# Cross attention in a decoder layer: keys and key steps turned side by side in one tile

## The chip, the core and the metric

The kernel runs on one NeuronCore of one Trainium2 chip. A core has TensorE (PE in the profile, PEld is its weight load), VectorE (DVE), ScalarE (ACT), GpSimd (POOL) and SyncE (SP), whose queue issues all transfers here. Times are device microseconds (us) of the whole program; lower is better.

## The reference, cut to what matters

One decoder layer on 32 batch elements of 100 rows by 256: a retention block, a cross attention, a feed-forward block, each with layer norm and residual. The change lies in the cross attention alone.

```python
kv_r = _apply_rope(kv_c, sin_k[None], cos_k[None])       # 1444 keys of 64 for each batch element
q_r = jnp.einsum('bshq,hqr->bhsr', q_big, W_qr)
k_r = jnp.einsum('bld,hdr->bhlr', kv_r, W_kr)
scores = jnp.einsum('bhsr,bhlr->bhsl', q_r, k_r)
attn = jax.nn.softmax(scores, axis=-1)
ctx_c = jnp.einsum('bhsl,bld->bhsd', attn, kv_r)
ctx_lat = jnp.einsum('bhsd,hkd->bhsk', ctx_c, w_kc_kv)
ctx = ctx_lat.transpose(0, 2, 1, 3).reshape(Bv, Sv, H * K)
return ctx @ Wo.T
```

There are 16 heads, so 1600 query rows meet 1444 keys in each batch element.

## The kernel before

An earlier phase leaves in device memory the rotated keys (`d["kr"]`), the differences of a key and its predecessor in another chunk (`d["kd"]`, called steps here), and the queries folded with W_kr, in a rounded part (`qh`) and a rest (`ql`).

The cross phase (`phase_cross_attention`) goes over the 32 batch elements in **slots**, one each, with an extra slot -1 ahead. A slot n does two things at once: the attention of element n, and the row maxima of element n + 1, which need rounded keys `kh`. It has 12 **chunks** c = 0 to 11 of 120 or 121 keys. For every chunk TensorE makes scores in two halves (`scores`, L1872), by adding to the scores in PSUM those of the chunk's steps (`dh` rounded, `dl` the rest; products dh by qh, dl by qh, dh by ql). ScalarE takes the exponentials (L1688), TensorE multiplies the chunk before with the values (`context`, L1892), and GpSimd adds the exponentials up (L1667), which gives the denominators.

Between these stand the **units** of the PSUM ring, which has two banks (0 and 1). `Ring` gives each single unit the next bank in turn; a unit waits until what was last in its bank has been read:
- `max` (L1940): two matmuls, both banks, read by one VectorE reduction (L1793).
- `half` twice (L1947): one matmul and bank each; the first is read by VectorE (L1802), the second is copied out by ScalarE (L1712), then reduced by VectorE (L1806).
- `kT` 0, 1, 2 (L1900): four transposes each; a third of the keys turned to 64 by keys. The tile `kr` holds each key twice side by side, so the turned keys stand in partitions 0 to 63 and again in 64 to 127, where the two halves of the queries need them. ScalarE copies them to `kh` (L1696).
- `dT` 0, 1, 2 (L1900): the same for the steps (`kd`, chunk 0 from `kr`); ScalarE copies to `dh` (L1703), VectorE subtracts for `dl` (L1770).
- `den` 0, 1 (L1925): sums of the denominators over partitions; ScalarE copies to `dens` (L1719).
- `mT` (L1952): the maxima, turned; they come back by way of device memory as `mq` for the first chunk of the next slot (L1879).
- `out` (L1931): the output product of the element before, 8 fp32 matmuls which the trace shows as 16; VectorE adds the residual (L1784).

TensorE's order is written by hand in `order`: out, dT 0 and kT 2 open chunk 0; dT 1 and 2 end chunk 2; den 0 and 1 end chunk 4; mT, kT 0 and kT 1 (for the element two slots on) end chunk 11. Chunks 0, 3 and 5 have no `half` pair; the last chunk's `max` is 466 wide, the others 512.

SyncE's queue runs `slot` in order: load_q, load_kv, load_xr, store_x2, load_qm, load_kr (two copies of the keys, after kT 2), load_kd (two copies of the steps, after dT 2), `invert`, load_m. `invert` (L1581) stores the denominators of the element before, waits, loads them as 100 by 16 (`few`), waits for VectorE's reciprocal (L1776), stores that, waits, and loads it spread over partitions (`rden`). VectorE takes this reciprocal in order, after the reduction of chunk 6, wherever the load is by then. GpSimd's `normalise` (L1653) multiplies context and `rden` after it has added chunk 9.

Of the kernel before, what the change touches and what calls it, by code (L numbers as in the profile page):

```python
# [18 lines left out]
L, DC = 1444, 64  # L19
# [1278 lines left out]
class Ring:  # L1298
# [18 lines left out]
    def count(self, units, where, keys=None):  # L1317

        totals = {("filled", i): 0 for i in range(2)} | {("read", i): 0 for i in range(3)}
        for n, u in enumerate(units):  # L1320
            totals["filled", self.banks[u][-1]] += 1
            totals["read", self.reader(u)] += 1
            where[keys[n] if keys else u] = dict(totals)
        return totals
# [48 lines left out]
def phase_cross_attention(nc, d, ahead):  # L1373


    with ExitStack() as ctx:
# [17 lines left out]
        kd = sb("kd", [LP, LC - 1, 2, DC])  # L1394
# [43 lines left out]
        first_max, *_, last_max = [u for u in units if u[0] == "max"]  # L1438
        copied = [u for u in units if u[0] == "half" and u[3] == 1]
        last_steps = [u for u in units if u[0] == "dT"][-2:]  # L1440


        def made(n, u):
            if u[0] == "kT":
# [7 lines left out]
        ends += [(B, ("out",)), (B, ("den", 0)), (B, ("den", 1)), (B + 1, ("out",))]  # L1452
        rg = Ring(ctx, nc, "x_ring", units, [("kT", 0), ("kT", 1)], ends, B - 2)
# [18 lines left out]
        kr_loaded = sig("kr_loaded", 32)  # L1472
        kd_loaded = sig("kd_loaded", 32)
# [6 lines left out]
        dh_copied = sig("step_high_copied", 3, 3)  # L1480
# [37 lines left out]
        def _(sp):  # L1518

            def load_kr(n):  # L1520

                if not is_at(n, 0):
                    wait_filled(sp, n - 2, ("kT", 2))
                rows = d["kr"][bass.ds(n, 1)].rearrange("b p (c e) -> (b p) c e", e=DC)
                for side in range(2):
                    sp.dma_start(kr[:, :, side], rows).then_inc(kr_loaded.sem, 16)

            def load_kd(n):

                if not is_at(n, 0):  # L1530
                    wait_filled(sp, n - 2, ("dT", 2))
                rows = d["kd"][bass.ds(n, 1)].rearrange("b p (c e) -> (b p) c e", e=DC)
                for side in range(2):
                    sp.dma_start(kd[:, :, side], rows).then_inc(kd_loaded.sem, 16)
# [62 lines left out]
            def slot(n, parity):  # L1597
# [22 lines left out]
            load_kd(0)  # L1620
# [16 lines left out]
        def _(pool):  # L1637
# [9 lines left out]
            def normalise(n):  # L1647
# [3 lines left out]
                wait_filled(pool, n, ("out",))  # L1651
# [24 lines left out]
        def _(act):  # L1676
# [14 lines left out]
            def copy_keys(n, i):  # L1691

                u = ("kT", i)
                wait_filled(act, n, u)
                a, b = span[i]
                act.copy(kh[:, a:b], ring[:, rg.banks[u][0], 0:b - a]).then_inc(read_sem(u), 1)  # L1696

            def copy_steps(n, parity, i):

                u = ("dT", i)  # L1700
                wait_filled(act, n, u)
                a, b = span[i]
                act.copy(dh[:, parity, a:b], ring[:, rg.banks[u][0], 0:b - a]).then_inc(dh_copied.sem, 1)  # L1703
# [23 lines left out]
            def slot(n, parity):  # L1727

                def singles(units):
                    for u in units:  # L1730
                        if not made_at(n, u):
                            continue
                        if u[0] == "kT":
                            copy_keys(n, u[1])
                        elif u[0] == "dT":
                            copy_steps(n, 1 - parity, u[1])
                        elif u[0] == "den":
                            save_den(n, u[1])

                for c in range(LC):  # L1740
# [3 lines left out]
                    if c == 0:  # L1744
                        singles(beside[c])
# [3 lines left out]
                    if c > 0:  # L1749
                        singles(beside[c])  # L1750
                    elif not is_at(n, -1) and not is_at(n, 0):
                        save_context(n)

            for i in range(2):
                copy_keys(-2, i)
# [6 lines left out]
        def _(dve):  # L1762
            ahead.wait(dve)

            def low_steps(n, parity, i):

                dve.wait_ge(dh_copied.sem, dh_copied.at(n, i + 1))
                u = ("dT", i)
                a, b = span[i]
                dve.tensor_tensor(dl[:, parity, a:b], ring[:, rg.banks[u][0], 0:b - a], dh[:, parity, a:b].bitcast(F32),  # L1770
                                  ALU.subtract).then_inc(read_sem(u), 1)
# [72 lines left out]
        def _(pe):  # L1844
# [15 lines left out]
            def scores(n, parity, c, u):  # L1860
# [35 lines left out]
            def turn(bank, i, chunk):  # L1896
# [480 lines left out]
```

## Time and profile before

| | us |
|---|---|
| three runs: lowest, median, highest | 2560.36, 2560.82, 2561.19 |
| the profiled execution, its own time | 2560.71 |
| its span, first to last instruction | 2558.9 |
| outside the span | 1.8 |
| cross phase, slots 0 to 30 (of the span) | 1479.5 |
| granted TensorE clock, mean | 0.964 |

The 1.8 us outside the span are a constant. The slots 0 to 30 begin with the first scores at 837.53 and end at 2317.05; slot 31 has no maxima to make. A row of a timeline gives start, duration, engine, line, operation and tiles; "[0.33 <-DVE x_x L1784]" is the idle time ahead of it and who ended that.

### The profile page before, as it was taken

To read this page: it belongs to the slowest core of one execution; us is meant where nothing else is said; L and a number is where in the kernel's file an instruction comes from. 1 tells how busy PE (TensorE), PEld (TensorE's weight loads), DVE (VectorE), ACT (ScalarE), POOL (GpSimd) and SP (SyncE) were. 2 spreads that over 40 slices of the span, in tenths; PEclk is the share of its full clock that TensorE was granted. 3 is DMA by queue.
4 is the path that set the end of the run, shared out by engine and by line. 5 is a ranking of instruction groups with operands and counts; after the bars stand their busy time and mean duration, and the time that the engine had idled before them with its cause. 6 is when DMAs were issued, how large, how long until landed. Compare 5 with 4: busy or idle time off the path is not lost. (4 is left out here: it accounts for less than half of the span.)

```text
span 2558.9 us, 47949 instructions
## 1 busy us (share of the span) xinstructions
PE 2353.3 (92%) x15794; PEld 1493.1 (58%) x15794; DVE 1620.2 (63%) x2689; ACT 1178.7 (46%) x1893; POOL 1840.6 (72%) x827
## 2 busy tenths in 40 slices
PE   7889858999985999999999999999999999999398
PEld 4455446777752555555555555555555555555288
DVE  5898857888855556556566566556565565561475
ACT  3232321222221556566565555555555555664143
POOL 2445526988871788888888888888888888889111
PEclk9999978999996999999999999999999999999699
DMA  4000016666653432332332432432432432410111
GB/s 132 14 22 22 13 51 177 185 173 183 183 162 83 87 78 64 90 76 64 91 75 64 94 72 64 94 74 61 96 75 59 98 74 58 98 46 13 39 46 39
DMA packets 310370, 210.37 MB, mean 82 GB/s; under 512 B 200054, under 2 KB 289354, under 8 KB 310176
## 3 DMA queue, kind: packets, MB, share of 16 engines
q1 hardware_dynamic: 310304, 209.51, 33.2%
q8 instruction: 38, 0.62, 0.1%
q14 instruction: 28, 0.23, 0.0%
HBM read 149.98 MB, written 59.48 MB: 82 GB/s over the span
## 5 line engine op out<-in xcount | busy, mean ns | idle before, releaser
L1667 POOL TENSOR_TENSOR x_acc<-x_acc,x_prob 120x1600 f32<-120x1600 f32 (+1 forms) x320 | 1153.1, 3603 | 42.8 <-ACT x_prob L1688 20.2
L1688 ACT ACTIVATE x_prob<-x_scores 120x800 f32<-120x800 f32 (+1 forms) x768 | 602.1, 837 | 41.6 <-PE x_scores L1872 19.7
L1892 PE MATMUL x_context<-x_prob,x_kv 120*64 120x400 f32 (+1 forms) x3072 | 600.4, 512 | 0.0
L1793 DVE TENSOR_REDUCE x_mx<-x_ring 115x2 f32<-115x1024 f32 (+2 forms) x384 | 467.7, 1218 | 202.3 <-PE x_ring L1940 189.8
L1892 PEld LDWEIGHTS x_context<-x_prob,x_kv 120*64 120x64 f32 (+1 forms) x3072 | 186.3, 136 | 254.1 <-issue 237.0
L1712 ACT COPY x_half<-x_ring 115x466 f32<-115x466 f32 (+2 forms) x288 | 153.4, 533 | 318.3 <-PE x_ring L1947 318.3
L1802 DVE TENSOR_REDUCE x_mx<-x_ring 115x1 f32<-115x466 f32 (+2 forms) x288 | 179.1, 622 | 182.7 <-PE x_ring L1947 182.7
L1872 PE MATMUL x_scores<-x_qh,x_dh 64*120 64x400 f32 (+1 forms) x1536 | 276.0, 355 | 0.0
L1872 PE MATMUL x_scores<-x_ql,x_dh 64*120 64x400 f32 (+1 forms) x1536 | 266.4, 341 | 0.0
L1872 PE MATMUL x_scores<-x_qh,x_dl 64*120 64x400 f32 (+1 forms) x1536 | 265.6, 341 | 0.0
L1667 POOL TENSOR_TENSOR x_acc<-x_prob 121x1600 f32<-121x1600 f32 x32 | 115.3, 3603 | 172.1 <-ACT x_prob L1688 172.1
L1806 DVE TENSOR_REDUCE x_mx<-x_half 115x1 f32<-115x466 f32 (+2 forms) x288 | 177.9, 618 | 12.7 <-ACT x_half L1712 11.8
L1940 PE MATMUL x_ring<-x_kh,x_qm 64*115 64x512 f32 (+2 forms) x768 | 161.4, 414 | 16.5 <-DVE x_dl L1770 7.7
L1947 PEld LDWEIGHTS x_ring<-x_kh,x_qm 64*115 64x115 f32 (+1 forms) x576 | 51.2, 175 | 191.6 <-DVE x_mx L1793 191.6
L1872 PEld LDWEIGHTS x_scores<-x_qh,x_dh 64*120 64x120 f32 (+1 forms) x1536 | 140.2, 178 | 36.6 <-issue 29.9
L1931 PE MATMUL x_ring<-x_wco,x_ctxn 128*100 128x256 f32 x560 | 135.8, 398 | 20.5 <-POOL x_ctxn L1653 14.6
L1947 PE MATMUL x_ring<-x_kh,x_qm 64*115 64x466 f32 (+2 forms) x576 | 134.2, 462 | 13.2 <-DVE x_mx L1793 13.2
L1872 PEld LDWEIGHTS x_scores<-x_qh,x_dl 64*120 64x120 f32 (+1 forms) x1536 | 140.3, 178 | 6.1
L1784 DVE TENSOR_TENSOR x_x<-x_ring,x_xr 100x256 f32<-100x256 f32 x35 | 14.8, 424 | 200.5 <-PE x_ring L1931 200.5
L1872 PEld LDWEIGHTS x_scores<-x_ql,x_dh 64*120 64x120 f32 (+1 forms) x1536 | 140.4, 178 | 1.1
L1215 PE MATMUL q_pp<-q_rot,q_ac 128*64 128x400 f32 x768 | 136.2, 503 | 1.0 <-issue 1.0
L1146 DVE TENSOR_TENSOR q_rot<-q_pq,q_cosq 128x400 f32<-128x400 f32 (+1 forms) x192 | 109.6, 571 | 31.1 <-PE q_pq L1203 28.0
(177 smaller groups left out, 3739.9 us busy)
## 6 DMA issues: line engine op xcount, KB each, us to landing
x_kr<-scratch_kr SPq DMA_DIRECT2D x64, 363.0 KB
x_kd<-scratch_kd SPq DMA_DIRECT2D x64, 332.8 KB
x_rden<-scratch_rden SPq DMA_DIRECT2D x68, 200.0 KB, 3.5
scratch_qh<-q_qsh SPq DMA_DIRECT2D x64, 200.0 KB, 3.8
scratch_ql<-q_qsl SPq DMA_DIRECT2D x64, 200.0 KB, 3.8
x_qm<-scratch_qh SPq DMA_DIRECT2D x64, 200.0 KB, 4.1
x_qh<-scratch_qh SPq DMA_DIRECT2D x64, 200.0 KB, 3.4
x_ql<-scratch_ql SPq DMA_DIRECT2D x64, 200.0 KB, 3.8
```

The source lines that it names most:

```text
L1215: mm = pe.matmul(pp[DC * side:DC * side + DC, p % 2, 0:GT], ac[:, 2 * p + side, j], rot[:, p % 4, 3 * side + j], start=j == 0, stop=j == 2)
L1667: pool.tensor_tensor(acc[0:rows, parity], first, prob[0:rows, c % PR], ALU.add).then_inc(acc_done.sem, 1)
L1688: act.activation(prob[0:rows, c % PR, u * HALF:(u + 1) * HALF].rearrange("p (j s) -> p j s", j=2), psc[0:rows, u, :, 0:BANK], ACT.Exp).the ...
L1712: act.copy(half[rows, k % 2, 0:b - a], ring[rows, rg.banks[u][0], 0:b - a]).then_inc(read_sem(u), 1)
L1793: dve.tensor_reduce(best[0:block_rows(r), :, r, i], ring[0:block_rows(r), :, 0:b - a], AX.X, ALU.max).then_inc(read_sem(u), 1)
L1802: dve.tensor_reduce(to, ring[0:block_rows(r), rg.banks[u][0], 0:b - a], AX.X, ALU.max).then_inc(read_sem(u), 1)
L1806: dve.tensor_reduce(to, half[0:block_rows(r), copied.index(u) % 2, 0:b - a], AX.X, ALU.max).then_inc(half_read.sem, 1)
L1872: mm = pe.matmul(psc[0:rows, u, j, 0:BANK], k[part, parity, a:a + rows], q[part, parity, cols], start=c == 0 and k is dh and q is qh, stop ...
L1892: mm = pe.matmul(pav[DC * s:DC * s + DC, j, 0:BANK], kv[0:rows, parity, c], prob[0:rows, c % PR, cols], start=c == 0, stop=c == LC - 1)
L1931: mm = pe.matmul(ring[0:S, bank, 0:E], ctxn[:, h // 4, (h % 4) * S:(h % 4 + 1) * S], wco[:, h], start=h == 0, stop=h == H // 2 - 1)
L1940: mm = pe.matmul(ring[0:block_rows(r), t, 0:b - a], qm[part, 1 - parity, r * MR:r * MR + block_rows(r)], kh[part, a:b], start=True, stop=True)
L1947: mm = pe.matmul(ring[0:block_rows(r), bank, 0:b - a], qm[part, 1 - parity, r * MR:r * MR + block_rows(r)], kh[part, a:b], start=True, sto ...
```

## The change

- `kr` holds in its two columns of 64 a key and its step, no longer the key twice. The tile `kd` is gone. A unit `turn` i replaces kT i and dT i: four transposes put keys in partitions 0 to 63 and steps in 64 to 127 of one bank.
- ScalarE copies the steps to dh[64:128], waits for VectorE, copies the keys to kh[0:64]. VectorE copies the keys to kh[64:128], waits for ScalarE, subtracts to dl[64:128]. A turn's bank is free when both are through.
- The lower halves of dh and dl are filled by two transfers within on-chip memory, `double_steps`, on SyncE's queue after `invert`.
- turn 2 ends chunk 4, after den 0 and 1. turn 0 and 1 end chunk 11. The unit out stands behind mT in chunk 11, ahead of them, and so handles its element at the end of a slot, not at the start of the next.
- Chunk 0 has no ring unit. Chunk 3 has a `half` pair; the last `max` is 512 wide.
- load_kr makes three transfers (keys, steps, the keys of chunk 0 once more) after turn 2; load_kd is gone.

```diff
-    own = [("out",), ("dT", 0), ("kT", 2)] if c == 0 else []
-    if c not in (0, 3, 5):
+    own = []
+    if c not in (0, 5):
         r, i = next(narrow)
         own += [("half", r, i, 0), ("half", r, i, 1)]
-    own += [("scores", 0), ("scores", 1), next(wide) if c < LC - 1 else ("max", *next(narrow)), ("context",)]
-    own += {2: [("dT", 1), ("dT", 2)], 4: [("den", 0), ("den", 1)],
-            LC - 1: [("mT",), ("kT", 0), ("kT", 1)]}.get(c, [])
+    own += [("scores", 0), ("scores", 1)]
+    if c > 0:
+        own.append(next(wide))
+    own.append(("context",))
+    own += {4: [("den", 0), ("den", 1), ("turn", 2)],
+            LC - 1: [("mT",), ("out",), ("turn", 0), ("turn", 1)]}.get(c, [])
...
 def load_kr(n):
     if not is_at(n, 0):
-        wait_filled(sp, n - 2, ("kT", 2))
+        wait_filled(sp, n - 2, ("turn", 2))
     rows = d["kr"][bass.ds(n, 1)].rearrange("b p (c e) -> (b p) c e", e=DC)
-    for side in range(2):
-        sp.dma_start(kr[:, :, side], rows).then_inc(kr_loaded.sem, 16)
-
-def load_kd(n):
...
+    steps = d["kd"][bass.ds(n, 1)].rearrange("b p (c e) -> (b p) c e", e=DC)
+    sp.dma_start(kr[:, :, 0], rows).then_inc(kr_loaded.sem, 16)
+    sp.dma_start(kr[:, 1:, 1], steps).then_inc(kr_loaded.sem, 16)
+    sp.dma_start(kr[:, 0, 1], rows[:, 0]).then_inc(kr_loaded.sem, 16)
+
+def double_steps(n, parity):
+    wait_read(sp, n - 1, ("turn", 2))
+    for t in (dh, dl):
+        sp.dma_start(t[0:DC, parity].bitcast(F32), t[DC:P, parity].bitcast(F32)
+                     ).then_inc(steps_doubled.sems[parity], 16)
...
     if further:
         load_qm(n + 2, parity)
         load_kr(n + 2)
-        load_kd(n + 2)
     invert(n)
     if not last:
+        double_steps(n + 1, 1 - parity)
         load_m(n + 1, 1 - parity)
...
+def copy_turn(n, parity, i):                      # ScalarE
...
+    act.copy(dh[DC:P, parity, a:b], ring[DC:P, bank, 0:b - a]).then_inc(dh_copied.sem, 1)
+    act.wait_ge(kh_copied.sem, kh_copied.at(n, (2, 3, 1)[i]))
+    act.copy(kh[0:DC, a:b], ring[0:DC, bank, 0:b - a]).then_inc(read_sem(u), 1)
...
+def take_turn(n, parity, i):                      # VectorE
...
+    dve.tensor_copy(kh[DC:P, a:b], ring[0:DC, bank, 0:b - a]).then_inc(kh_copied.sem, 1)
+    dve.wait_ge(dh_copied.sem, dh_copied.at(n, (2, 3, 1)[i]))
+    dve.tensor_tensor(dl[DC:P, parity, a:b], ring[DC:P, bank, 0:b - a],
+                      dh[DC:P, parity, a:b].bitcast(F32), ALU.subtract).then_inc(read_sem(u), 1)
```

SyncE's queue in the loop over slots, before, from the loads of keys on (ISA and REGISTER_ALU rows are waits and their values):

```order
L1526 DMA x_kr<-scratch_kr 121x12x64 x2
L59 REGISTER_ALU
L1534 ISA
L1534 DMA x_kd<-scratch_kd 121x11x64 x2
L59 REGISTER_ALU
L1585 DMA scratch_den<-x_dens 2x800
L1587 ISA
L1588 DMA x_few<-scratch_den 100x16
L1590 DMA scratch_rden<-x_few 100x16
L1593 DMA x_rden<-scratch_rden 64x800 x2
L59 REGISTER_ALU
L1575 DMA scratch_m<-x_mrow 14x115
```

The same place in the changed kernel:

```order
L1529 DMA x_kr<-scratch_kr 121x12x64
L1530 ISA
L1530 DMA x_kr<-scratch_kd 121x11x64
L1531 DMA x_kr<-scratch_kr 121x64
L59 REGISTER_ALU
L1589 DMA scratch_den<-x_dens 2x800
L1591 ISA
L1592 DMA x_few<-scratch_den 100x16
L1594 DMA scratch_rden<-x_few 100x16
L1597 DMA x_rden<-scratch_rden 64x800 x2
L59 REGISTER_ALU
L1537 DMA x_dh<-x_dh 64x1444
```

The key loads still stand ahead of the chain of `invert`, but what they wait for has moved from chunks 0 and 2 to the end of chunk 4, where the denominators come too.

TensorE's queue from the end of one slot to the first scores of the next, before (two transposes or more of a shape make one row):

```order
L1952 MATMUL x_ring<-x_ident,x_negm 14x115
L1912 ISA
L1900 MATMUL x_ring<-x_ident,x_kr 128x121 x4
L1900 MATMUL x_ring<-x_ident,x_kr 128x120 x4
L59 REGISTER_ALU
L59 ISA
L1931 MATMUL x_ring<-x_wco,x_ctxn 100x256 x4
L59 REGISTER_ALU
L1931 MATMUL x_ring<-x_wco,x_ctxn 100x256 x4
L1900 MATMUL x_ring<-x_ident,x_kr 128x121
L1900 MATMUL x_ring<-x_ident,x_kd 128x121 x3
L59 ISA
```

and in the changed kernel:

```order
L1939 MATMUL x_ring<-x_ident,x_negm 14x115
L59 ISA
L1920 MATMUL x_ring<-x_wco,x_ctxn 100x256 x4
L59 REGISTER_ALU
L1920 MATMUL x_ring<-x_wco,x_ctxn 100x256 x4
L59 REGISTER_ALU
L1906 ISA
L1892 MATMUL x_ring<-x_ident,x_kr 128x121 x4
L59 REGISTER_ALU
L1892 MATMUL x_ring<-x_ident,x_kr 128x120 x4
L1857 ISA
L1859 ISA
```

Sixteen transposes stood there (four more 128x120 follow the excerpt of before); eight stand there now, behind the output product.

VectorE's queue around the reciprocal, before (chunks 4 to 7):

```order
L1793 TENSOR_REDUCE x_mx<-x_ring 115x2 x2
L1802 TENSOR_REDUCE x_mx<-x_ring 115x1
L1806 TENSOR_REDUCE x_mx<-x_half 115x1
L1793 TENSOR_REDUCE x_mx<-x_ring 115x2
L1776 RECIPROCAL x_few<-x_few 100x16
L1802 TENSOR_REDUCE x_mx<-x_ring 115x1
L1806 TENSOR_REDUCE x_mx<-x_half 115x1
L1793 TENSOR_REDUCE x_mx<-x_ring 115x2
```

and in the changed kernel:

```order
L1785 TENSOR_REDUCE x_mx<-x_ring 110x2
L1760 CAST x_kh<-x_ring 64x480
L1762 TENSOR_TENSOR x_dl<-x_ring,x_dh 64x480
L1785 TENSOR_REDUCE x_mx<-x_ring 115x2
L1794 TENSOR_REDUCE x_mx<-x_ring 115x1
L1798 TENSOR_REDUCE x_mx<-x_half 115x1
L1785 TENSOR_REDUCE x_mx<-x_ring 115x2
L1768 RECIPROCAL x_few<-x_few 100x16
L1794 TENSOR_REDUCE x_mx<-x_ring 115x1
```

The reciprocal has kept its place after the reduction of chunk 6; a key copy and a subtraction for turn 2 stand two chunks ahead of it.

## Rows read from the trace of the kernel before

**Rows 1.** One whole slot by stretches: busy of each engine, clock, DMA share, GB/s.
```profile
1459.17:1507.05 47.88, 47.18 (x336) 27.92 (x335) 28.45 (x38) 28.32 (x42) 41.56 (x14) 1.00 0.33 73
```

**Rows 2.** Timeline of all engines, from mT of that slot to the next slot.
```profile
1500.73 1.15 PE L1900 MATMUL x_ring<-x_ident,x_kr 121*128 121x121 f32 x8
...
1502.07 3.69 PE L1931 MATMUL x_ring<-x_wco,x_ctxn 128*100 128x256 f32 x16 [0.19 <-ACT x_kh L1696]
...
1506.02 0.42 DVE L1784 TENSOR_TENSOR x_x<-x_ring,x_xr 100x256 f32<-100x256 f32 x1 [4.82 <-PE x_ring L1931]
1506.22 0.56 ACT L1703 CAST x_dh<-x_ring 128x484 fp32r<-128x484 f32 x1 [3.74 <-PE x_ring L1900]
...
1506.49 0.63 PE L1900 MATMUL x_ring<-x_ident,x_kr 120*128 120x120 f32 x4 [0.31 <-DVE x_x L1784]
1506.82 0.66 DVE L1770 TENSOR_TENSOR x_dl<-x_ring,x_dh 128x484 fp32r<-128x484 f32 x1 [0.38 <-ACT x_dh L1703]
```

**Rows 3.** Timeline of TensorE within the slot that begins at 1459.17.
```profile
1460.73 0.40 PE L1940 MATMUL x_ring<-x_kh,x_qm 64*115 64x512 f32 x2
1461.06 1.56 PE L1892 MATMUL x_context<-x_prob,x_kv 120*64 120x400 f32 x8
1462.56 0.45 PE L1947 MATMUL x_ring<-x_kh,x_qm 64*115 64x420 f32 x2
...
1464.04 0.49 PE L1940 MATMUL x_ring<-x_kh,x_qm 64*115 64x512 f32 x2
...
1469.20 1.04 PE L1900 MATMUL x_ring<-x_ident,x_kd 120*128 120x120 f32 x8
...
1473.65 0.45 PE L1947 MATMUL x_ring<-x_kh,x_qm 64*115 64x420 f32 x2
...
1478.33 0.44 PE L1872 MATMUL x_scores<-x_qh,x_dh 64*120 64x400 f32 x2
...
1481.35 0.47 PE L1947 MATMUL x_ring<-x_kh,x_qm 64*115 64x466 f32 x2
```

**Rows 4.** Timeline of ScalarE, chunks 0 and 1 of that slot.
```profile
1460.20 1.57 ACT L1688 ACTIVATE x_prob<-x_scores 121x800 f32<-121x800 f32 x2 [0.36 <-PE x_scores L1879]
1462.75 0.83 ACT L1725 COPY x_ctxs<-x_context 128x800 f32<-128x800 f32 x1 [0.97 <-PE x_context L1892]
1463.47 0.52 ACT L1712 COPY x_half<-x_ring 115x420 f32<-115x420 f32 x1
```

**Rows 5.** Timeline of SyncE's queue, that slot; a duration is that of the issue.
```profile
1470.41 2.83 SPq L1534 DMA_DIRECT2D x_kd<-scratch_kd  x2
1478.96 0.57 SPq L1585 DMA_DIRECT2D scratch_den<-x_dens  x1
1480.66 0.30 SPq L1588 DMA_DIRECT2D x_few<-scratch_den  x1
```

**Rows 6.** Timeline of VectorE: its reciprocal in that slot, and in slot 31.
```profile
1484.33 0.24 DVE L1776 RECIPROCAL x_few<-x_few 100x16 f32<-100x16 f32 x1
...
2336.56 0.25 DVE L1776 RECIPROCAL x_few<-x_few 100x16 f32<-100x16 f32 x1 [18.99 <-DMA x_few<-scratch_den]
```

**Rows 7.** SyncE's queue in slots -1 and 31: issues with nothing else under way.
```profile
795.38 1.75 SPq L1534 DMA_DIRECT2D x_kd<-scratch_kd  x2
...
2335.04 0.27 SPq L1588 DMA_DIRECT2D x_few<-scratch_den  x1
```

**Rows 8.** A stretch after that load of steps in slot -1 (columns of rows 1).
```profile
797.00:801.00 4.00, 1.90 (x6) 0.56 (x4) 2.41 (x3) 0.51 (x1) 0.00 (x0) 0.50 0.81 168
```

**Rows 9.** Timeline of GpSimd in the slot that begins at 1459.17.
```profile
1499.23 2.07 POOL L1653 TENSOR_TENSOR x_ctxn<-x_ctxs,x_rden 128x400 f32<-128x400 f32 x2
```

**Rows 10.** Timeline of TensorE, slot -1 and the end of the phase.
```profile
776.39 1.01 PE L1900 MATMUL x_ring<-x_ident,x_kr 121*128 121x121 f32 x8 [2.07 <-DMA x_kr<-scratch_kr]
...
786.28 0.70 PE L1947 MATMUL x_ring<-x_kh,x_qm 64*115 64x420 f32 x2 [1.32 <-DVE x_mx L1793]
...
2365.66 1.56 PE L1925 MATMUL x_ring<-x_acc,x_ones 121*64 121x400 f32 x8 [1.76 <-POOL x_acc L1667]
```

More of the change, by code:

```diff
@@ L1321, in count @@
             totals["filled", self.banks[u][-1]] += 1
-            totals["read", self.reader(u)] += 1
+            totals["read", self.reader(u)] += 2 if u[0] == "turn" else 1
             where[keys[n] if keys else u] = dict(totals)
@@ L1437, in phase_cross_attention @@
         units = [u for own in beside for u in own]
-        first_max, *_, last_max = [u for u in units if u[0] == "max"]
+        first_max, *_ = [u for u in units if u[0] in ("max", "half")]
+        *_, last_max = [u for u in units if u[0] == "max"]
         copied = [u for u in units if u[0] == "half" and u[3] == 1]
-        last_steps = [u for u in units if u[0] == "dT"][-2:]
         def made(n, u):
-            if u[0] == "kT":
+            if u[0] == "turn":
                 return n + (2 if u[1] < 2 else 1) <= B - 1
@@ L1451, in phase_cross_attention @@
         ends = [(n, u) for n in (B - 2, B - 1) for u in units if made(n, u)]
-        ends += [(B, ("out",)), (B, ("den", 0)), (B, ("den", 1)), (B + 1, ("out",))]
-        rg = Ring(ctx, nc, "x_ring", units, [("kT", 0), ("kT", 1)], ends, B - 2)
+        ends += [(B, ("den", 0)), (B, ("den", 1)), (B, ("out",))]
+        rg = Ring(ctx, nc, "x_ring", units, [("turn", 0), ("turn", 1)], ends, B - 2)
         def wait_filled(eng, n, u):
@@ L1689, in exponentials @@
                                psc[0:rows, u, :, 0:BANK], ACT.Exp).then_inc(exp_done.sem, 1)
-            def copy_keys(n, i):
-                u = ("kT", i)
+            def copy_turn(n, parity, i):
+                u = ("turn", i)
                 wait_filled(act, n, u)
                 a, b = span[i]
[L1696 to L1703, printed above, removed]
+                bank = rg.banks[u][0]
+                act.copy(dh[DC:P, parity, a:b], ring[DC:P, bank, 0:b - a]).then_inc(dh_copied.sem, 1)
+                act.wait_ge(kh_copied.sem, kh_copied.at(n, (2, 3, 1)[i]))
+                act.copy(kh[0:DC, a:b], ring[0:DC, bank, 0:b - a]).then_inc(read_sem(u), 1)
             def copy_half(n, u):
@@ L1727, in slot @@
             def slot(n, parity):
[L1729 to L1738, printed above, removed]
                 for c in range(LC):
@@ L1748, in slot @@
                             exponentials(n, c, u)
[L1749 to L1752, printed above, removed]
+                        if c == 0 and not is_at(n, 0):
+                            save_context(n)
+                    for u in beside[c]:
+                        if u[0] == "den":
+                            save_den(n, u[1])
+                        elif u[0] == "turn" and made_at(n, u):
+                            copy_turn(n, parity if u[1] < 2 else 1 - parity, u[1])
             for i in range(2):
-                copy_keys(-2, i)
+                copy_turn(-2, 0, i)
             in_turn(act, slot)
@@ L1837, in _ @@
             dve.wait_ge(memset.sem, N_MEMSET)
+            for i in range(2):
+                take_turn(-2, 0, i)
             in_turn(dve, slot)
-            output(B, 0)
             invert(B)
@@ L1866, in scores @@
                     pe.wait_ge(q_loaded.sems[parity], q_loaded.done(n, parity))
-                    for step in last_steps:
-                        wait_read(pe, n - 1, step)
+                    pe.wait_ge(steps_doubled.sems[parity], steps_doubled.done(n, parity))
                 for k, q in ((dh, qh), (dl, qh), (dh, ql)):
@@ L1894, in context, with turn @@
                 mm.then_inc(av_done.sem, 1)
-            def turn(bank, i, chunk):
+            def turn(bank, i):
                 a = span[i][0]
@@ L1900, in turn @@
                     mm = pe.transpose(ring[:, bank, b:b + rows],
-                                      chunk(rows, c), ident[0:rows, 0:rows])
+                                      kr[0:rows, c].rearrange("p s e -> p (s e)"), ident[0:rows, 0:rows])
                 return mm
@@ L1971, in _ @@
             for i in range(2):
-                make(-2, 0, ("kT", i))
+                make(-2, 0, ("turn", i))
             in_turn(pe, slot)
             context(B - 1, 1, LC - 1)
-            for u in (("out",), ("den", 0), ("den", 1)):
+            for u in (("den", 0), ("den", 1), ("out",)):
                 make(B, 0, u)
-            make(B + 1, 1, ("out",))
 def layout_cross(i):
```

55 lines of the change are left out of this document (20 added, 35 removed).

## The prediction

> **What bounds the kernel now.** I read first the stretches of one slot, to see whose busy time fills it: TensorE works 47.18 of 47.88 us at granted clock 1.00, GpSimd 41.56, VectorE and ScalarE some 28 each [rows 1]. Slots repeat: the first scores of slots 0 and 31 stand at 837.53 and 2317.05, 31 slots in 1479.5, most of them 47.8 long. So the cross phase, 58% of the span, is bound by TensorE, and a wait counts only if TensorE sits in it. Then I read TensorE's timeline for such waits, the other engines' for what they would be late with, and SyncE's queue. I write T for the first scores of a slot (1459.17 in the rows) and T' for the same place in the changed kernel.
>
> **The part that is removed.** From mT to the next scores TensorE ran, besides mT, eight transposes (kT 0, 1) from 1500.73 to 1502.07, then the output product, then eight more with a wait of 0.31 for the residual add, until 1507.05 [rows 2]. Now eight stand where sixteen did, and turn 1 still waits for the bank of out. The first piece, 1.34 with its wait of 0.19, goes; from out to the next scores the 4.98 (1502.07 to 1507.05) stay.
> Chunk 2's eight transposes and chunk 3, with the wait behind them, took 1469.20 to 1473.65, 4.45 [rows 3]. Now that is one chunk with a half pair. Chunks 6 to 11, six of that kind, took 19.28 (from 1481.35 to mT, 0.10 before 1500.73), so 3.21 each [rows 2, 3]: 1.24 saved. The count of reductions stays, but for one pair of halves in place of the narrow last max; its price is in that 3.21.
>
> **Chunks 0 and 1.** Chunk 0 loses its max, 0.33 (1460.73 to 1461.06), so the half pair of chunk 1 may begin at T' + 3.06, before T + 3.39 [rows 3]. But ScalarE and VectorE now have four passes each to make on turns 0 and 1 where they had two or three, each waiting for the other. A pass of 484 columns takes 0.56 on ScalarE and 0.66 on VectorE [rows 2]. A copy to other partitions by VectorE is in no row; the subtraction of the same size, 0.66, is nearest; half of it and twice it are my bounds. VectorE adds the residual until T' - 0.61, copies keys until +0.10, subtracts until +0.79, then the same for turn 1 until +2.13. ScalarE's last key copy ends at +2.09; its exponentials take 1.57 [rows 4] and end at +3.7, its save of the context at 4.5, the copy of the half at 4.9. The max of chunk 1 begins at T' + 5.0 instead of the T + 4.87 of before. Chunk 0's gain is thus eaten: chunk 2 ends 0.08 later than before. With VectorE's copy at twice its price it would be 0.5 to 1 more; at half, 0.3 less.
>
> **Chunks 4 and 5.** Turn 2 adds four transposes, 0.55, behind the denominators. Its bank is read by VectorE until about T' + 19.96 (fill 18.6, twice 0.66), and chunk 5's max wants it at 19.75: wait 0.27, and 0.1 for the restart. Sum up to the end of chunk 5: before T + 22.18, now 22.18 + 0.08 - 1.24 + 0.55 + 0.35 = T' + 21.92. If nothing more happened, the slot would last 21.92 + 19.38 (chunks 6 to 11 and mT) + 0.1 (a wider last max ahead of mT) + 4.98 = 46.38, a **gain of 1.50**.
>
> **What the move of the loads costs.** SyncE now issues the key loads behind turn 2, directly ahead of `invert`. Turn 2 is filled at T' + 18.63; SyncE issued 0.17 after such a fill (1469.20 + 1.04 to 1470.41) [rows 3, 5]: 18.80. Into idle transfer engines two step loads were issued in 1.75 [rows 7], with the small third load about 2.1: the store of the denominators follows at 20.9 instead of T + 19.8. That alone is covered. But 726 KB lie ahead of it. In slot -1 two step loads of 333 KB began to move 1.6 after their first issue and ran at 168 GB/s [rows 7, 8]. So the key loads drain at 18.80 + 1.62 + 4.33 = T' + 24.75. Before, chunks 2 to 4 hid this: the steps, issued at T + 11.2, had long drained when the store came at T + 19.8.
> How long the store then needs is in no row, since none stands behind a queue. Alone it needed 1.70 from issue to the next issue, 1.13 after its own issue time [rows 5]. Behind the drain it cannot need more than 1.70, and not less than nothing; I take 0.9, near the 1.13, since the confirmation of a write comes after the data in any case. The load of `few` is then issued at 25.65 and needs 1.52 to the reciprocal (2335.04 to 2336.56) [rows 6, 7]: T' + 27.17.
> VectorE comes to the reciprocal at T' + 24.9 (T + 25.16 before [rows 6]), and everything of its own queue stands behind it: the first half reduction of chunk 7, 0.64, whose bank chunk 7's max needs at T' + 26.54. It gets it at 27.17 + 0.24 + 0.64 + 0.05 = 28.10. **TensorE waits 1.56** there, where it had no wait. VectorE then needs 2.5 of each 3.2 and catches up before chunk 9. The slot: 46.38 + 1.56 + 0.1 (restart) = 48.04 against 47.88, **+0.16**, over the 30 slots with key loads +5.
> GpSimd's products for out begin at T + 40.06 and take 2.07 [rows 9]; fed by exponentials as early as before, they are ready when out asks at T' + 42.9, and would just be ready without the stall. The doubled steps (740 KB) are issued at about T' + 30, behind the inverses; at the 168 GB/s of rows 8 they land by 36, 12 ahead of their first use: nothing. The maxima come back some 4 after mT and are asked for 5.5 after it: nothing, cover 1.5.
> The Trainium skill, "DMA: Bandwidth & Descriptors", section "Queues, rings and completion order", says that each transfer engine takes descriptors in ring order and that a completion lands only after all earlier writes of that engine. No row here shows it; it would give the case that I forecast, and nothing of the sum is taken from it. The same page, "Why small descriptors are slow", finds no penalty for small pieces between on-chip memories; no row shows such a transfer.
>
> **Start and end.** In slot -1 the first half pair stood at 786.28, behind out, the steps' load and their turns; now it may follow the turns of 776.39 [rows 10] after their passes, at 779.8: -6.5. The rest is estimated from the timeline of that slot at half clock: -3.2 (no second turns), +1.5 (half pair in chunk 3), +2 (turn 2), +1.4 (the same stall), and -1.3 at its end: about -6 in all. At the end of the phase an output product now precedes the last context product, both at half clock behind GpSimd, so the last denominators start some 1.2 after 2365.66 [rows 10]. Sum: 2560.7 - 6 + 5 + 1.2 = 2560.9, put at **2561**, since the profiled execution's 2560.71 is the median within 0.1.
>
> **Rivals.**
> (a) The store is not held up: it overtakes, or only some of the 16 transfer engines have a backlog. Then `few` comes at 24.2, before VectorE asks, and each slot gains 1.50: 2561 - 30 x 1.66 = 2511. For it: the den store is tiny; against it: one queue issues all, and its engines are over 80% busy in such a load [rows 8]. Chance 0.13.
> (b) Slower: the store pays its whole 1.70 behind the drain, `few` arrives at 27.97 and TensorE waits 2.36: +0.96 a slot, 2585. For it: a write that must be confirmed; against it: its issue and the fetching of its descriptors lie in the backlog's time. It decides from a reciprocal at T' + 27.3 on, from where each further 0.1 costs 3 us in all. A key load at 140 GB/s instead of 168 drains 0.9 later and gives 2587. Chance 0.24.
> (c) The turn's double reading is dearer than I take it (VectorE's copy to other partitions at twice 0.66): 0.7 a slot, 2582. Chance 0.08, slower too.
> The forecast, the stall that gives the gain back, has 0.55, spread from 2545 to 2577, since 0.4 in the reciprocal's time and 0.2 in chunk 1 are open in each of 30 slots.
>
> **The numbers.** A measurement of this kernel can tell about 0.2%, 5 us, from no change. Of my 0.55, 0.23 lie below 2555.7, 0.22 within, 0.10 above 2565.9. With rivals: faster 0.36, same 0.22, slower 0.42. The range, 2530 to 2592, leaves out (a) and some 0.06 of tails. The likeliest case alone: 2545 to 2577.
>
> **What would show it.** In the changed kernel: slots of 47.9 to 48.2; an idle time of VectorE ahead of the reciprocal of 2 to 2.5, put down to the load of `few`; one of 1.3 to 1.8 on TensorE ahead of the max of chunk 7; the key loads issued just ahead of the store of the denominators and 4 to 5 from there to the issue of `few`, where 1.70 stood; no 0.19 ahead of out; 0.3 ahead of chunk 5's max, 0.5 ahead of chunk 1's. Wrong would be: slots of 46.4 without idle time at the reciprocal (rival a), or idle time ahead of the first scores of a slot, where neither steps nor maxima should be late.

## The result: 0.3% slower, the saving given back in one wait

| | before | after |
|---|---|---|
| runs: lowest, median, highest | 2560.36, 2563.82, 2567.13 (11 runs) | 2566.88, 2570.01, 2581.22 (11 runs) |
| the profiled execution, its own time | 2560.71 | 2568.1 |
| its span | 2558.9 | 2566.3 |
| first scores of slot 0 | 837.53 | 830.51 |
| first scores of slot 31 | 2317.05 | 2324.06 |
| last denominators start | 2365.66 | 2372.69 |

The ratio is 1.0029, with a 95% interval of 1.0017 to 1.0042: slower, by 0.2 to 0.4%. The predicted 2561 lies 9 under the median of after and 7 under its profiled execution, on which kind of time the sum was built; the range of 2530 to 2592 holds both. (The eleven runs of before have a median 3 above that of the three from which I forecast.)

The three last rows of the table give the account of the difference of the spans, 7.4: the start of the phase gives 7.0 back, the end costs 0.0 (48.63 from slot 31 to the last denominators, before 48.61), and the 31 slots between grew by 14.0. The 0.4 that is missing lies behind the last denominators (193.6 to the end of the span, before 193.2).

First the stretches of a slot, to be set against [rows 1]. The columns are the stretch and its length, the busy time (and instructions) of TensorE, its weight loads, VectorE, ScalarE and GpSimd, then granted clock, DMA share, GB/s. These are two slots in succession:

```profile
1413.50:1461.90 48.40, 45.99 (x312) 26.17 (x309) 29.29 (x40) 27.62 (x42) 40.84 (x13) 0.96 0.32 73
1461.90:1509.50 47.60, 45.82 (x323) 26.48 (x324) 30.41 (x41) 28.63 (x43) 41.07 (x14) 1.00 0.32 74
```

TensorE's work fell from 47.18 to 45.82 in a slot at full clock; the slot is 47.60 long instead of 47.88. What was saved stands idle. The first of the two has clock 0.96, which no slot of before had in the middle of the phase; more on that below.

TensorE's and VectorE's timelines of that second slot and the next one tell where the idle time is. A row gives start, duration, engine, line, operation and tiles, and in brackets the idle time ahead and what ended it; L1927 is the `max` unit, L1794 the reduction of the first `half`, L1785 that of a `max`, L1768 the reciprocal:

```profile
1485.41 1.23 DVE L1785 TENSOR_REDUCE x_mx<-x_ring 115x2 f32<-115x1024 f32 x1
1488.74 0.25 DVE L1768 RECIPROCAL x_few<-x_few 100x16 f32<-100x16 f32 x1 [2.10 <-DMA x_few<-scratch_den]
1488.91 0.58 DVE L1794 TENSOR_REDUCE x_mx<-x_ring 115x1 f32<-115x466 f32 x1
...
1489.54 0.48 PE L1927 MATMUL x_ring<-x_kh,x_qm 64*115 64x512 f32 x2 [1.19 <-DVE x_mx L1794]
...
1537.72 0.49 PE L1927 MATMUL x_ring<-x_kh,x_qm 64*115 64x512 f32 x2 [1.75 <-DVE x_mx L1794]
```

VectorE has finished chunk 6's reduction and stands 2.10 for `few`, where [rows 6] has no idle time; the half of chunk 7 waits behind it in program order, and TensorE waits for that bank. Over the 30 slots that load keys the groups of waits read so (total us, times, longest):

```profile
DVE x_few L1768 <- DMA x_few<-scratch_den: 73.5, 30, 3.4
```

with 46.2 in 30 waits of TensorE's `max` for L1794, 1.54 each. VectorE's are 2.45 each, so the slot shown (2.10 and 1.19) is one of the milder ones. The next waits of TensorE in that list are 0.3 and 0.2 a slot.

SyncE's queue of the same slot shows why `few` is late, against [rows 5]. A duration is that of the issue:

```profile
1480.35 0.88 SPq L1529 DMA_DIRECT2D x_kr<-scratch_kr  x1
1481.42 1.29 SPq L1530 DMA_DIRECT2D x_kr<-scratch_kd  x1
1482.81 1.78 SPq L1531 DMA_DIRECT2D x_kr<-scratch_kr  x1
1484.71 0.57 SPq L1589 DMA_DIRECT2D scratch_den<-x_dens  x1
1487.26 0.29 SPq L1592 DMA_DIRECT2D x_few<-scratch_den  x1
```

and the stretches around it, in the columns above:

```profile
1482.00:1484.00 2.00, 2.00 (x14) 0.88 (x14) 1.23 (x1) 0.91 (x2) 1.60 (x2) 1.00 0.74 170
1484.00:1486.00 2.00, 2.00 (x20) 1.30 (x18) 1.78 (x3) 1.88 (x3) 2.00 (x1) 1.00 0.91 167
1486.00:1488.00 2.00, 2.00 (x18) 1.31 (x16) 0.64 (x1) 0.87 (x3) 1.92 (x2) 1.00 0.20 37
```

The key loads move at some 170 GB/s until about 1486.4, and `few` is issued 0.86 after that. From the issue of the store of the denominators to that of `few` it is 2.55, before 1.70.

The mean of 31 slots, mT to mT, is 48.27. But they fall into two kinds: 26 of 46.1 to 48.4 (the 46.1 is the last, which loads no keys; the other 25 are 47.98 in the mean), and five of 50.81, 50.34, 49.85, 49.72 and 49.91. The five are those in which the granted clock fell behind the wait. Below stand the wait at 1440.21, which had such a fall behind it (the one at 1489.54 above had none), and then the 6.70 us that begin 0.3 behind the wait's end, for four slots at the start of the phase:

```profile
1440.21 0.49 PE L1927 MATMUL x_ring<-x_kh,x_qm 64*115 64x512 f32 x2 [1.71 <-DVE x_mx L1794]
...
1442.86 0.53 PE L1864 MATMUL x_scores<-x_qh,x_dh 64*120 64x400 f32 x2
```

```profile
858.68:865.38 6.70, 6.70 (x38) 3.02 (x38) 3.73 (x5) 2.07 (x3) 4.29 (x2) 0.79 0.71 170
908.99:915.69 6.70, 6.70 (x36) 3.21 (x36) 3.80 (x5) 2.07 (x3) 3.59 (x2) 0.75 0.74 169
958.76:965.46 6.70, 6.70 (x52) 3.85 (x52) 5.11 (x8) 3.43 (x6) 5.93 (x2) 1.00 0.65 167
1006.71:1013.41 6.70, 6.70 (x52) 3.87 (x52) 5.14 (x8) 3.45 (x6) 6.31 (x3) 1.00 0.69 168
```

With clock 0.75 or 0.79 TensorE got through 36 to 38 recorded matmuls where it makes 52 at 1.00; the scores took 0.53 a pair instead of 0.34. The clock stands at 0.50 (the 1.2 GHz level) for half of such a stretch and is then full again. A slot with that is about 1.9 longer than the mean of the others (49.85 against 47.98), but its wait is longer too. A slot less its own wait of TensorE is 46.52 in the mean of the 25 without a fall (46.45 to 46.60, whatever the wait) and 48.07 in the mean of four with one (the first slot of the phase left out, since in before too it is 1.1 longer): a fall costs 1.55.

### The profile page after: what moved, and what is told of

The parts are those of the page before. It is cut to its first block and busy times, and to the rows that moved or that the text cites. A ratio compares the mean times of both kernels' runs of the same rounds, so it can differ in the third digit from the quotient of the medians.

```text
span 2566.3 us, 47308 instructions
## 1 busy us (share of the span) xinstructions
PE 2317.2 (90%) x15394; PEld 1447.2 (56%) x15394; DVE 1686.8 (66%) x2816; ACT 1189.1 (46%) x1925; POOL 1839.7 (72%) x827
## 5 line engine op out<-in xcount | busy, mean ns | idle before, releaser
L1785 DVE TENSOR_REDUCE x_mx<-x_ring 115x2 f32<-115x1024 f32 (+1 forms) x352 | 431.5, 1226 | 52.8 <-PE x_ring L1927 35.3
L1711 ACT COPY x_half<-x_ring 115x420 f32<-115x420 f32 (+2 forms) x320 | 171.5, 536 | 403.4 <-PE x_ring L1934 403.4
L1794 DVE TENSOR_REDUCE x_mx<-x_ring 115x1 f32<-115x420 f32 (+2 forms) x320 | 197.8, 618 | 222.2 <-PE x_ring L1934 222.2
L1927 PE MATMUL x_ring<-x_kh,x_qm 64*115 64x512 f32 (+1 forms) x704 | 151.9, 426 | 63.0 <-DVE x_mx L1794 54.0
L1798 DVE TENSOR_REDUCE x_mx<-x_half 115x1 f32<-115x420 f32 (+2 forms) x320 | 197.9, 618 | 15.0 <-ACT x_half L1711 13.1
L1934 PEld LDWEIGHTS x_ring<-x_kh,x_qm 64*115 64x115 f32 (+1 forms) x640 | 57.3, 176 | 215.5 <-DVE x_mx L1785 188.5
L1934 PE MATMUL x_ring<-x_kh,x_qm 64*115 64x466 f32 (+2 forms) x640 | 150.7, 467 | 14.8 <-DVE x_mx L1785 11.9
L1700 ACT CAST x_dh<-x_ring 64x480 fp32r<-64x480 f32 (+1 forms) x96 | 53.4, 556 | 178.5 <-PE x_ring L1892 175.9
```

What stands on the lines that cost most here:

```text
L1711: act.copy(half[rows, k % 2, 0:b - a], ring[rows, rg.banks[u][0], 0:b - a]).then_inc(read_sem(u), 1)
L1785: dve.tensor_reduce(best[0:block_rows(r), :, r, i], ring[0:block_rows(r), :, 0:b - a], AX.X, ALU.max).then_inc(read_sem(u), 1)
L1794: dve.tensor_reduce(to, ring[0:block_rows(r), rg.banks[u][0], 0:b - a], AX.X, ALU.max).then_inc(read_sem(u), 1)
L1798: dve.tensor_reduce(to, half[0:block_rows(r), copied.index(u) % 2, 0:b - a], AX.X, ALU.max).then_inc(half_read.sem, 1)
L1927: mm = pe.matmul(ring[0:block_rows(r), t, 0:b - a], qm[part, 1 - parity, r * MR:r * MR + block_rows(r)], kh[part, a:b], start=True, stop=True)
L1934: mm = pe.matmul(ring[0:block_rows(r), bank, 0:b - a], qm[part, 1 - parity, r * MR:r * MR + block_rows(r)], kh[part, a:b], start=True, sto ...
```

## The experiments

Theory: the store of the denominators stands behind 726 KB on one queue; `few` comes late; VectorE's program order hands that to TensorE. Rivals: the wait comes from what VectorE or ScalarE now do more (the double reading of a turn); or the loads slow something by their traffic rather than by their place in the queue. The slots without a wait should then still be 48. Every kernel was timed beside before (median 2564.78 for experiments 1 to 4, 2565.32 for 5 to 7), and all ratios are to it. After itself is 1.0029.

**1. The store ahead of the loads.** In after, `invert` is cut in two; its first half (store, wait, load of `few`) goes ahead of the key loads.

```diff
     if further:
         load_qm(n + 2, parity)
-        load_kr(n + 2)
     invert(n)                        # now ends with the load of few
+    if further:
+        load_kr(n + 2)
+    spread_inverses(n)               # the rest of invert
```

> The changed kernel, but SyncE stores the denominators and loads them back as few ahead of the key loads; the spreading of the inverses stays behind them. Theory Q (few waits behind the queued key loads, VectorE waits in order for few, TensorE for VectorE): no idle time at the reciprocal, none of the 1.2 to 2.5 us ahead of chunk 7's max, slots of 46.4 instead of the 48.3 of the changed kernel's mean, clock 1.00 all through the slots, about 2510 us. Rival P (the doubled passes over the turned banks on ScalarE and VectorE cost the time, the queue is a bystander): the slots stay near 48 and the time near 2565.

Measured: 2509.52 (2503.95 to 2511.0), ratio 0.9783, interval 0.9767 to 0.9799. Slots are 46.2 to 46.4. SyncE's queue, and VectorE at the reciprocal (here L1774):

```profile
1498.06 0.60 SPq L1589 DMA_DIRECT2D scratch_den<-x_dens  x1
1499.78 0.30 SPq L1592 DMA_DIRECT2D x_few<-scratch_den  x1
1500.35 0.89 SPq L1529 DMA_DIRECT2D x_kr<-scratch_kr  x1
...
1503.28 1.23 DVE L1791 TENSOR_REDUCE x_mx<-x_ring 115x2 f32<-115x1024 f32 x1
1504.42 0.24 DVE L1774 RECIPROCAL x_few<-x_few 100x16 f32<-100x16 f32 x1
```

The store needs 1.72 again, as alone [rows 5], and the reciprocal follows without idle time. All computing and every byte moved are those of after, and 60 us are gone. The double reading is no cause.

**2. VectorE takes the reciprocal later.** SyncE's order stays; the reciprocal stands behind chunk 7's reductions.

```diff
-                    if c == 6:
+                    if c == 7:
                         invert(n)
```

> The changed kernel, but VectorE takes the reciprocal after chunk 7 instead of after chunk 6; SyncE's queue is as in the changed kernel, so few comes as late as there. Theory Q: VectorE gets to it at about 28.1 us after the slot's first scores, few is there at 27.4, so no wait, slots of 46.4, about 2510 us. Rival C (the transfers themselves slow the engines in chunk 7, by contention, not by the order on VectorE): the wait of TensorE at chunk 7 stays, 2565 us.

Measured: 2507.64 (2507.34 to 2511.43), ratio 0.9785 (0.9769 to 0.9802), the fastest median of all. `few` is as late as in after, and nobody waits for it:

```profile
1501.25 0.58 SPq L1589 DMA_DIRECT2D scratch_den<-x_dens  x1
1503.82 0.29 SPq L1592 DMA_DIRECT2D x_few<-scratch_den  x1
...
1504.94 1.23 DVE L1785 TENSOR_REDUCE x_mx<-x_ring 115x2 f32<-115x1024 f32 x1
1506.09 0.24 DVE L1768 RECIPROCAL x_few<-x_few 100x16 f32<-100x16 f32 x1
```

and one slot, in the columns of [rows 1]:

```profile
1477.30:1523.55 46.25, 45.64 (x323) 26.53 (x323) 30.71 (x42) 28.56 (x43) 41.72 (x14) 1.00 0.35 81
```

The traffic and its place in the queue are those of after, so neither costs TensorE anything by itself. It is the reciprocal's place in VectorE's order, with the lateness, that makes the wait. Removing either end of the chain gives the same 2508 to 2510.

**3. A longer queue.** A fourth load of 363 KB, of keys into a tile that nobody reads, between the key loads and the store. (KB are of 1024 bytes, as the profile counts them.)

```diff
+                sp.dma_start(spare[:], rows).then_inc(kr_loaded.sem, 16)
```

> The changed kernel with one more load of the same keys (363 KB, 1452 pieces of 256 bytes) into a spare tile, issued right ahead of the store of the denominators. Theory Q: at 168 GB/s the queue drains 2.2 us later, the wait at the reciprocal grows from 2.4 to 4.6 us, that of TensorE from 1.5 to 3.7; +65 us for 30 slots, and more slots in which the clock falls, so 2635 to 2690 us. Rival I (only the time in which SyncE issues counts, not the drain): +0.9 a slot, about 2597 us. Rival P: no change.

Measured: 2672.38 (2670.07 to 2676.37), ratio 1.0426 (1.0409 to 1.0444).

```profile
1532.54 0.57 SPq L1591 DMA_DIRECT2D scratch_den<-x_dens  x1
1536.40 0.29 SPq L1594 DMA_DIRECT2D x_few<-scratch_den  x1
...
1537.90 0.25 DVE L1770 RECIPROCAL x_few<-x_few 100x16 f32<-100x16 f32 x1 [3.90 <-DMA x_few<-scratch_den]
...
1538.71 0.49 PE L1929 MATMUL x_ring<-x_kh,x_qm 64*115 64x512 f32 x2 [2.98 <-DVE x_mx L1796]
```

TensorE's wait went from 1.54 to 3.3 in the mean, so 1.8 more for 363 KB, where 168 GB/s would give 2.2. The expectation took this load for 1452 pieces of 256 bytes like the others, but its destination is a tile without gaps: the trace has 121 pieces of 3 KB, and they moved faster.

```profile
1534.00:1535.50 1.50, 1.50 (x16) 1.19 (x14) 0.01 (x1) 0.80 (x2) 1.42 (x2) 1.00 0.60 201
```

At 201 GB/s the 363 KB take 1.85, which is the 1.8. Slots grew by more than that, from 48.3 to 51.3. The rest is the clock: it fell behind 27 of the 30 waits (of 2.7 to 4.1), in after behind 5 of 30 (of 1.0 to 2.5). Two stretches of 6.70, taken as above, behind waits of 3.13 and 3.77:

```profile
1125.71:1132.41 6.70, 6.70 (x38) 3.62 (x38) 3.80 (x5) 2.18 (x3) 3.17 (x2) 0.75 0.71 167
1021.88:1028.58 6.70, 6.70 (x30) 3.45 (x30) 3.01 (x5) 2.05 (x3) 1.55 (x1) 0.56 0.71 168
```

Six of the 27 falls are of the second kind, about twice as long: clock 0.54 to 0.60 in the stretch. Five of them stand behind waits of 3.72 to 4.09, the sixth behind the 3.36 of the first slot. A slot less its wait is 46.53 without a fall (3 slots), 48.10 with a short one (21) and 49.37 with a long one (5): 1.57 and 2.84 each.

So the length of the queue ahead of the store sets the wait, and the wait brings a second cost.

**4. The same queue in the kernel before.** No turns side by side, no second reading; only the load of the steps (two copies, 666 KB) waits for the denominators' unit instead of dT 2.

```diff
-                    wait_filled(sp, n - 2, ("dT", 2))
+                    wait_filled(sp, n - 2, ("den", 1))
```

> The kernel before, with one edit: its two loads of steps (666 KB) wait for the denominators' product at the end of chunk 4 and not for dT 2 at the end of chunk 2, so they stand directly ahead of the store of the denominators. Nothing else of the change is in it. Theory Q: few lands at about 27.4 us after the slot's first scores, VectorE wanted it at 25.2, TensorE waits 1.5 at chunk 7: slots of 49.3 instead of 47.8, 2607 us, up to 2625 if the clock falls too. Rival P: no change from 2561.

Measured: 2630.95 (2625.88 to 2631.96), ratio 1.0255 (1.0238 to 1.0273).

```profile
1511.20 1.78 SPq L1534 DMA_DIRECT2D x_kd<-scratch_kd  x2
1513.03 2.14 SPq L1585 DMA_DIRECT2D scratch_den<-x_dens  x1
1517.97 0.30 SPq L1588 DMA_DIRECT2D x_few<-scratch_den  x1
...
1519.57 0.25 DVE L1776 RECIPROCAL x_few<-x_few 100x16 f32<-100x16 f32 x1 [2.54 <-DMA x_few<-scratch_den]
```

Moving one load in front of the store reproduces both: waits of TensorE of 1.2 to 1.85, 1.55 in the mean, and the falls of the clock, behind 6 of the 30 waits. Slots went from 47.85 to 49.9. A slot less its wait is 48.08 without a fall and 49.66 with one, again 1.6. The DMA share in the 6.7 us behind these waits was 0.18 to 0.25, where it was some 0.7 in after; the falls come with either traffic.

**5. Half of the queue behind the store.** In after, only the steps' load (333 KB) goes behind `invert`; 393 KB stay ahead.

```diff
     if further:
         load_qm(n + 2, parity)
         load_kr(n + 2)               # keys, and the keys of chunk 0
     invert(n)
+    if further:
+        load_steps(n + 2)
```

> The changed kernel with its load of steps (333 KB) issued behind invert; the loads of keys (394 KB) stay ahead of the store of the denominators. Theory Q: half the backlog, so it drains 18.45 + 1.6 + 2.35 = 22.4 us after the slot's first scores, few is issued at 23.3 and there at 24.8, when VectorE asks at 24.9: no wait or 0.1, slots of 46.3 to 46.5, no fall of the clock, 2508 to 2515 us. If the wait went with the issue alone, or with anything that stands ahead of the store, it would be halved: slots of 47.1, 2535 us.

Measured: 2509.85 (2509.13 to 2511.45), ratio 0.9783 (0.9766 to 0.9799).

```profile
1500.32 0.59 SPq L1592 DMA_DIRECT2D scratch_den<-x_dens  x1
1502.55 0.29 SPq L1595 DMA_DIRECT2D x_few<-scratch_den  x1
```

The store still takes 2.23, and VectorE still waits for `few`, 9.7 in 22 times, 0.4 each. Behind the first slot those with up to 0.72 of it are 46.4 or less; the one with 1.00 is 46.58. The wait has a point from which it costs, as the prediction had it: VectorE may be some 0.7 late and still gives the bank back in time.

**6. All key loads last.** They go behind `invert` and the doubled steps.

```diff
-        load_kr(n + 2)
     invert(n)
     if not last:
         double_steps(n + 1, 1 - parity)
+    if further:
+        load_kr(n + 2)
+    if not last:
         load_m(n + 1, 1 - parity)
```

> The changed kernel with all three key loads issued behind invert and behind the doubling of the steps, so nothing is queued ahead of the denominators. Theory Q: as the first run with the store ahead, slots of 46.3, about 2509 us. Rival D (the keys have to be asked for by the end of chunk 4): they are issued near 31 us into the slot, drain near 37 and are turned at 44.7; only if they came later than that would TensorE wait ahead of turn 0.

Measured: 2508.45 (2508.06 to 2512.9), ratio 0.9782 (0.9766 to 0.9798). Now the doubled steps, 740 KB, are the queue that others stand behind, and it is the key loads that pay:

```profile
1508.16 1.03 SPq L1529 DMA_DIRECT2D x_kr<-scratch_kr  x1
1509.37 3.77 SPq L1530 DMA_DIRECT2D x_kr<-scratch_kd  x1
1513.23 2.28 SPq L1531 DMA_DIRECT2D x_kr<-scratch_kr  x1
...
1520.98 0.31 SPq L1579 DMA_DIRECT2D scratch_m<-x_mrow  x1
```

SyncE itself is held for 7 us, but the keys are wanted only behind out, and TensorE has no new wait. Experiments 1, 2, 5 and 6 differ by no more than their spread: once the wait is gone it makes no difference how.

**7. Another queue for the small transfers.** Experiment 3 with its 1089 KB, but ScalarE's queue issues the store (after its part of chunk 4) and the load of `few` (after chunk 5).

```diff
+                    if c == 4:
+                        store_den(n)
+                    if c == 5:
+                        load_few(n)
```

> The kernel with the extra load (2672 us, TensorE waiting 3.4 us a slot), but ScalarE issues the store of the denominators, at about 19.6 us, and the load of few, after chunk 5's exponentials; SyncE keeps the 1.1 MB of key loads. Theory E (the backlog is one of the 16 transfer engines, whichever queue issues): few still comes behind most of the drain, near 27, slots of 48 or more, 2560 to 2580 us. Theory S (it is SyncE's queue alone): few comes at 24 or earlier, no wait, slots of 46.3, 2510 us.

Measured: 2536.58 (2530.64 to 2537.05), ratio 0.9886 (0.987 to 0.9903): against experiment 3 with the same bytes 136 less, but 28 above the kernels without a wait. It lies between the cases. ScalarE's queue and VectorE:

```profile
1464.93 0.50 ACTq L1721 DMA_DIRECT2D scratch_den<-x_dens  x1
...
1468.05 0.29 ACTq L1728 DMA_DIRECT2D x_few<-scratch_den  x1
1468.51 0.51 ACT L1708 COPY x_half<-x_ring 115x420 f32<-115x420 f32 x1 [1.27 <-DMA scratch_den<-x_dens]
...
1471.43 0.25 DVE L1784 RECIPROCAL x_few<-x_few 100x16 f32<-100x16 f32 x1 [0.54 <-DMA x_few<-scratch_den]
```

```profile
1470.00:1472.00 2.00, 2.00 (x18) 1.15 (x16) 1.46 (x3) 0.90 (x2) 1.92 (x2) 1.00 0.70 194
```

The store took 3.1 from its issue to that of `few`, and `few` 3.4 to the reciprocal, where alone they take 1.70 and 1.5 [rows 5 to 7]; and both were done while the 1089 KB of the other queue were still moving. So the order of one queue is the larger part of the delay; a smaller part stays, and traffic under way on the same 16 engines is what is left to explain it. The Trainium skill, "DMA: Bandwidth & Descriptors", section "Queues, rings and completion order", says that every queue has a ring of its own on the same engines, each served in order, and that an engine takes packets from the rings in turn. The trace agrees: 3.1 and 3.4, neither the 1.70 and 1.5 of an idle queue nor the whole drain. Of the +28, ScalarE's own wait of 1.27 for the store and VectorE's of 0.66 are the visible part: TensorE waits 0.4 for `x_half` in 26 slots. In slots 0 to 30 of this kernel TensorE's waits were under 0.9 and the clock never fell behind one.

Not tried: the output product ahead of the turns by itself. It shares banks and waits with the turns, and no version with it behind them alone was run; its part in the saving isn't separated.

## Why the prediction was right, and where it was off

**The mechanism** was the forecast one, step by step. Times are from the first scores T' = 1461.90 of the slot shown, with the mean over the 30 slots that load keys beside them where it differs:

| step | forecast | measured |
|---|---|---|
| max of chunk 1 starts | 5.0, wait 0.5 | 4.64, wait 0.1 |
| end of chunk 5 | 21.92 | 21.7 |
| first key load issued | 18.80 | 18.45 |
| store issued | 20.9 | 22.8 (mean 23.06) |
| traffic drained | 24.75 | 24.5 |
| `few` issued, after the drain | 0.9 | 0.86 |
| `few` issued | 25.65 | 25.36 (mean 25.66) |
| reciprocal | 27.17 | 26.84 (mean 27.20) |
| TensorE's wait | 1.56 | 1.19 (mean 1.54) |
| lost to the restart behind it | 0.1 | 0.2 (46.52 less 46.29) |
| slot without the wait | 46.38 | 46.29 (experiments 1 and 2, 2508 and 2510) |
| slot with the wait, full clock | 48.04 | 47.98 (mean of 25, whose waits are 1.46) |
| slot -1 | -6 | -7.0 |
| end of the phase | +1.2 | 0.0 |

**Terms that were off without effect.** The issue of the three loads took 4.4, not 2.1: the third, of 30 KB, needs 1.78, in a stretch in which the transfer engines are 74 to 91% busy. I had taken the rates of an idle queue [rows 7]. It does nothing here, as the store is done only behind the drain anyway. Two sums were slightly off: the rate of 168 GB/s was applied to 726 KB as if of 1000 bytes (with 1024 it is 4.43, not 4.33), and the copy of the half, by its own terms, would have ended at 5.0 and not 4.9. The chunk 1 term was 0.4 too dear: ScalarE's last key copy ended at T' + 1.86 instead of 2.09, and the passes behind it (exponentials 1.56 from 1463.77, context 0.83 from 1465.24, half 0.52 from 1465.97) overlap by some 0.1 each, where I had added them up. The copy to other partitions by VectorE, in no row of before, takes

```profile
1462.52 0.65 DVE L1760 CAST x_kh<-x_ring 64x480 fp32r<-64x480 f32 x1
```

so the value taken from the subtraction (0.66) was right and rival (c) false. The end's +1.2 did not show. TensorE had waited 1.76 for GpSimd ahead of the last denominators [rows 10]; now it waits 0.21, so the output product went for the larger part into that wait:

```profile
2372.69 0.56 PE L1914 MATMUL x_ring<-x_acc,x_ones 121*64 121x400 f32 x2 [0.21 <-POOL x_acc L1670]
```

I had named no cover for it.

**The term that was missing** is the clock. The sum took TensorE's rate as given, 1.00 in a slot [rows 1], and only the wait as a cost. The kernel before has no idle time over 0.5 in such a slot; its one wait of 1.32, at 840.83 in slot 0, had no fall behind it. But its end of phase shows one, behind a longer wait:

```profile
2357.45 6.45 PE L1931 MATMUL x_ring<-x_wco,x_ctxn 128*100 128x256 f32 x16 [3.85 <-POOL x_ctxn L1653]
```

The same product took 3.69 in a slot [rows 2]; here the granted clock was 0.50 from 2356.26 on for 6.8 us. The prediction says "half clock" of that place and of slot -1, and did not carry it over to the wait that it forecast in every slot. The five falls cost 1.55 each, 7.8; without them the slots between the first scores of 0 and 31 would have grown by 6.3, and the forecast was 5 (the restart was 0.13 dearer in each slot, the slot without a wait 0.09 cheaper). The profiled execution would have had 2560.3 instead of 2568.1; the forecast was 2561. That it is so near is in part luck: the start and the end came out 2.2 better than forecast, the slots 1.3 worse. The falls may also account for the spread of after, 14 us over 11 runs where before has 7, since a run with more or fewer of them gains or loses 1.6 for each. That is not shown: the falls were counted in one execution of each kernel.

**The rivals.** (a) had 2511 and is false for the change as it stands: the store is held up by the whole queue. Its time is right to 3.4 us for the kernels that take the wait away. Experiment 7 shows the version of it in which another queue carries the store, and there it holds in part. (b), the whole 1.70 behind the drain, is false (0.86); the result is on its side of before by another way, 7.8 us in five slots. Slower had the largest of my three chances, 0.42, but mostly for (b). In the likeliest case's own range, centred on no change, only wait and passes were open; the idle time's second cost was in none of my cases.

**What beats both kernels**: after with the reciprocal behind chunk 7 (2507.64), or with the store ahead of the key loads (2509.52), 2.2% under before. The 1.50 a slot that the change saves are real; they were paid back by the place of a 6 KB transfer in a queue, and by the clock behind the wait that it made.

## What to carry to other kernels

When a bulk load is moved in a queue, look at what small transfer stands behind it and who takes its result in program order: the small one is done when the bulk has drained, plus a part of its own latency (0.86 of 1.70 here), and the remedy costs nothing at either end (issue the small one first, or let its consumer take it one step later). Cost such a load by its drain, not by its issue time. And price a new wait of TensorE, where it is the bounding engine, above its length: behind waits of 1.0 to 2.5 the clock fell in one slot of six, behind 2.7 to 4.1 in nine of ten, at 1.6 a time and 2.8 for the long falls.

## What the runs showed of the hardware that I had not expected

- **The clock falls behind short waits.** In steady slots at clock 1.00, a wait of TensorE was followed by a stretch at 0.50 (half of the next 6.70 us in most cases, nearly twice as much in six of experiment 3): in 5 of 30 slots of after (waits 0.98 to 2.47; those with a fall had 1.68 to 2.47, while 1.69, 1.75, 1.79 and 1.85 passed without), in 6 of 30 of experiment 4 (1.2 to 1.85; falls from 1.65 on), in 27 of 30 of experiment 3 (2.7 to 4.1), and never in experiments 1, 2, 5, 6 and 7, whose waits in these slots stayed under 1. A fall cost 1.55 to 1.6 of the slot, a long one 2.8, on top of the wait. What besides the length of the wait decides is open.
- **A queue with much under way can hold the issuing engine.** A load of 30 KB took 1.78 to issue behind 696 KB, and one of 333 KB took 3.77 behind the doubled steps, where two of 333 KB took 1.75 into an idle queue [rows 7]. It does not go by bytes alone: the fourth load of experiment 3, 363 KB in 121 pieces, took 0.30 right behind those 726 KB:

```profile
1530.29 1.70 SPq L1532 DMA_DIRECT2D x_kr<-scratch_kr  x1
1532.11 0.30 SPq L1533 DMA_DIRECT2D x_spare<-scratch_kr  x1
```

- **A second queue gets past most of a backlog.** A store and a load that need 1.70 and 1.5 alone needed 3.1 and 3.4 on ScalarE's queue while SyncE's had 1089 KB under way; on SyncE's own queue the store stood until all had drained.
